# Cross attention with four key groups: products, evictions and small sums placed in other steps of the slot

## The reference, cut to what matters

```
q = heads(x @ to_q_w)
h_g = softmax(q @ heads(ctx_g @ to_k_g_w)^T / sqrt(32)) @ heads(ctx_g @ to_v_g_w)   for g in txt, obj, oth, ip
out = merge(h_txt) + merge(h_obj) + merge(h_oth) + merge(h_ip)
out = out @ to_out_w + to_out_b + x
```

## Time and profile before

| | us |
|---|---|
| median of 3 runs (2660.23 to 2662.57) | 2661.45 |
| the profiled execution's own time | 2661.54 |
| its span, first to last instruction | 2659.5 |
| PE matmul busy / weight loads busy | 2547.6 / 1936.9 |
| ACT busy | 1726.6 |
| DVE busy | 1622.1 |
| POOL busy | 408.5 |

### The profile page before, as it was taken

One profiled execution on the slowest core, in us unless ns is written; L12 is line 12 of the kernel. 1 busy time (PEld: TensorE's weight loads), 2 busy tenths in 40 slices (PEclk: granted clock), 3 DMA queues, 4 the chain that ended last, 5 costly groups with the idle time before them and its releaser, 6 DMA issues.

```text
span 2659.5 us, 37570 instructions
## 1 busy us (share of the span) xinstructions
PE 2547.6 (96%) x13221; PEld 1936.9 (73%) x13221; DVE 1622.1 (61%) x2964; ACT 1726.6 (65%) x3832; POOL 408.5 (15%) x564
## 2 busy tenths in 40 slices
PE   7999999999999947999999999999999999999997
PEld 7999999999999934566666666666666666666664
DVE  3131111111111138888888888888888888888882
ACT  3232212212121117999999999999999999999993
POOL 0000000000000022122122122221221221221210
PEclk9999999999999978999999999999999999999999
DMA  7473333332323246566666566666666666666642
GB/s 213 131 228 130 118 114 116 108 117 106 120 103 119 79 110 134 106 134 139 126 139 142 117 146 138 118 145 140 121 139 140 126 134 134 135 138 127 137 99 65
DMA packets 256918, 341.14 MB, mean 128 GB/s; under 512 B 48466, under 2 KB 150994, under 8 KB 256730
## 3 DMA queue, kind: packets, MB, share of 16 engines
q1 hardware_dynamic: 203312, 275.82, 45.4%
q10 hardware_dynamic: 53418, 62.93, 6.7%
HBM read 186.60 MB, written 83.89 MB: 102 GB/s over the span
## 4 chain that ended last, share of the span: by engine, by line
PE 41%; DVE 14%; issue 5%; ACT 4%; DMA 0%; SPq 0%; DVEq 0%
PE m_ps L838 11%; PE s_ps L766 8%; PE o_ps L794 8%; PE m_ps L815 7%; PE st_ps L780 7%; DVE negmax L949 4%; DVE q_out L1000 2%; ACT probs L885 2%; DVE small L956 2%; DVE q_out L997 2%; DVE heads L1010 2%; ACT s_ps L893 2%; DVE heads L1015 1%; DVE neglse L982 1%; DVE neglse L980 0%
## 5 line engine op out<-in xcount | busy, mean ns | idle before, releaser
L893 ACT ACTIVATE s_ps<-s_ps,negmax 128x427 f32<-128x427 f32 x1280 | 761.4, 599 | 69.7 <-DVE small L956 69.5
L949 DVE TENSOR_REDUCE negmax<-s_ps 128x2 f32<-128x854 f32 x640 | 663.2, 1036 | 146.9 <-PE s_ps L766 145.5
L885 ACT ACTIVATE probs<-st_ps 128x1024 f32<-128x1024 f32 x640 | 662.1, 1035 | 87.8 <-PE st_ps L780 87.8
L766 PEld LDWEIGHTS s_ps<-kpack,qpack 96*128 96x128 f32 x1280 | 348.4, 312 | 203.9 <-issue 114.6
L766 PE MATMUL s_ps<-kpack,qpack 96*128 96x512 f32 x1280 | 450.2, 434 | 35.9 <-ACT s_ps L893 29.2
L433 PE MATMUL v_ps<-w_split,ctx_split 128*128 128x320 f32 (+2 forms) x3168 | 467.5, 309 | 0.0
L433 PEld LDWEIGHTS v_ps<-w_split,ctx_split 128*128 128x128 f32 (+2 forms) x3168 | 461.2, 183 | 4.7 <-issue 0.5
L416 PE MATMUL k_ps<-ctx_split,w_split 128*128 128x428 f32 (+1 forms) x2280 | 431.1, 350 | 8.3 <-DVE k_out L361 8.3
L416 PEld LDWEIGHTS k_ps<-ctx_split,w_split 128*128 128x128 f32 x2280 | 413.0, 189 | 23.8 <-issue 9.3
L780 PE MATMUL st_ps<-qpack,kpack 104*128 104x512 f32 x1280 | 410.2, 402 | 9.1 <-ACT probs L885 6.1
L361 DVE TENSOR_TENSOR k_out<-k_ps,k_out 128x427 fp32r<-128x427 f32 (+1 forms) x97 | 56.3, 581 | 540.0 <-ACT k_out L257 540.0
(11 more groups left out here) (54 smaller groups left out, 1458.5 us busy)
## 6 DMA issues: line engine op xcount, KB each, us to landing
kpack<-kT SPq DMA_DIRECT2D x240, 256.0 KB, 5.4
qpack<-q_out SPq DMA_DIRECT2D x240, 256.0 KB, 5.6
kT<-k_out ACTq DMA_DIRECT2D x160, 217.5 KB, 2.2
ctx_split_raw<-in_ctxT SPq DMA_DIRECT2D x128, 214.0 KB, 4.6
xs_raw<-in_xT SPq DMA_DIRECT2D x80, 256.0 KB, 5.7
out<-in_xT SPq DMA_DIRECT2D x80, 256.0 KB, 6.0
out_yT<-out SPq DMA_DIRECT2D x80, 256.0 KB, 3.3
v_ip_rows<-v_out ACTq DMA_DIRECT2D x48, 320.0 KB
```

Source lines behind the costliest of these rows:

```text
L766: last = nc.tensor.matmul(s_ps[:, n % 2, z, :], queries_of(r, j, t), kpack[0:ROWS_S, r, j, :], start=True, stop=True)
L885: nc.scalar.activation(probs[:, at:at + 2, :], st_ps[:, :, :], ACT.Exp).then_inc(p_done, 1)
L893: last = nc.scalar.activation(s_ps[:, n % 2, z, SMALL:TOK], s_ps[:, n % 2, z, SMALL:TOK], ACT.Exp, bias=negmax[:, r, IP, j, t:t + 1], accu ...
L949: nc.vector.tensor_reduce(negmax[:, r, IP, j, t0:t0 + 2], s_ps[:, n % 2, :, SMALL:TOK], AX_X, ALU.max, negate=True).then_inc(s_max, 1)
```

## The change

Nothing that is computed changes. The steps of PE's `queries` move from 5, 6, 7 to 6, 7 and step 0 of the next slot; those of `output` from 1, 2, 3 to 2, 3, 4. `values` moves from steps 0, 2, 4, 6 to steps 1, 3, 5, 7: in 3 and 7 it stays between the transposed scores and the other products, in 1 and 5 it comes last, behind the plain scores. On DVE `keep_queries` moves from step 0 to 1, `small_sums` of the second half from 1 to 0, `add_output` from 4 to 5. POOL's splits of x take one step later names. The ring of probabilities grows from six to eight slices, and `out` shrinks from two buffers to one.

```diff
-OR = 2
+OR = 1
 HR = 9
-PR = 6
+PR = 8
@@
-Q_STEPS = {5: (0, 7), 6: (7, 9), 7: (9, 15)}
-X_STEPS = {0: (0,), 1: (1,), 2: (2,), 3: (3,), 5: (4,)}
+Q_STEPS = {6: (0, 6), 7: (6, 9), 0: (9, 15)}
+X_STEPS = {1: (0,), 2: (1,), 3: (2,), 5: (3,), 6: (4,)}
@@
-Y_STEPS = {1: (0, 6), 2: (6, 8), 3: (8, 15)}
+Y_STEPS = {2: (0, 6), 3: (6, 9), 4: (9, 15)}
@@ PE
             def products_at(m, k):
 
-                if k in Q_STEPS and unit(m):
-                    queries(m, range(*Q_STEPS[k]))
+                u = m if k > 0 else m - 1
+                if k in Q_STEPS and unit(u):
+                    queries(u, range(*Q_STEPS[k]))
@@ PE, slot
                         scores_t(u, duo)
-                    if k % 2 == 0 and unit(m - 4):
+                    if k in (3, 7) and unit(m - 4):
                         values(m - 4, k // 2)
                     products_at(m, k)
                     u, p = pair_at(m, k + 1) if k + 1 < STEPS else pair_at(m + 1, 0)
                     if unit(u):
                         scores(u, p)
+                    if k in (1, 5) and unit(m - 4):
+                        values(m - 4, k // 2)
@@ DVE, slot
-                    if k == 0 and unit(m - 1):
+                    if k == 0 and unit(m - 3):
+                        small_sums(m - 3, 1)
+                    if k == 1 and unit(m - 1):
                         keep_queries(m - 1)
-                    if k == 1 and unit(m - 3):
-                        small_sums(m - 3, 1)
@@ DVE, slot
-                    if k == 4 and unit(m - Y_LAG):
+                    if k == 5 and unit(m - Y_LAG):
                         add_output(m - Y_LAG)
```

## The result

The kernel after takes 2750.9 us (median of 4 runs, 2747.5 to 2753.3) against 2661.7 for the kernel before (4 runs, 2660.2 to 2662.6). The ratio is 1.0331, with an interval of 1.0319 to 1.0344. The forecast said slower, by 33 us; it is slower by 89, and 2750.9 lies outside the range of 2664 to 2714. The profiled execution has a span of 2745.6 us, 86.1 more than before's 2659.5.

What follows compares the result with a forecast made beforehand. PE, ACT and DVE nearly level at 19.96 us a slot; after, a 20.44 us loop through the query packing. Steady slots 20.8 more, start 8, tail 4.3: 33 us on 2661.54, so 2694 us, range 2664 to 2714.

Steps and rivals of the forecast that it cites:

- the loop: One slot long: packing waits for eviction, eviction for products, products for pair 0, pair 0 for packing; 20.44 us against 19.96.
- the packing of 8.2 us: From SP's first packing issue to pair 0 of the unit: 8.2 us, bounds 8.0 and 8.5, against PE's 7.57 of work.
- the price of a wait: PE's wait for the packed queries, counted as its own length only; no clock loss was forecast.
- the start: The nine intervals before 1153.46, 177.6 us before: 8 us more, three of the 19.11 kind losing 1.3 each.
- The rival of other traffic or the logsumexp rows: Residual, x chunks or logsumexp rows make the packing 0.6 us longer: 47 us more, 2740 us; chance 0.08.
- slots with a new x: The 14 steady slots in which POOL splits a new x: 20.64 us each, 0.43 less than 21.07.
- the 19.11 kind: Early slots in which no output is made yet, 19.11 us before; three of them were to lose 1.3 us each.
- the sign I named, nearly the same period with and without outputs: Period between issues of L652 is 20.3 to 20.6, nearly the same with and without outputs, if the forecast is right.
- The tail, "4.3 more": Last outputs with one `out` buffer: 5.7 us apart instead of 4.62, four times, 4.3 us more.
- The rival in which the collision only moves to another chunk: POOL's split of the third chunk meets DVE's logarithms fully, by the lock: 8 us more, 2702 us; chance 0.10.
- Were this all, a slot would last some 19.7 us: The steady slot from the changes to PE's list and the eviction stall alone, without the packing loop: some 19.7 us.
- 0.24 us less for each slot: On PE, two pairs of scores behind a `values` become transposed pairs, 0.10 to 0.11 against 0.23 each: 0.24 us less.

Runs made afterwards that it cites:

- the shorter third transfer: The kernel after with the last of the three packing transfers cut to 128 of 512 tokens from unit 4 on: 2678.6 us, ratio 1.0064 against the kernel before.

## Why the prediction was wrong in size, step by step

The way and the loop were right. The time failed on three terms: the packing of 8.2 us, which took 8.43 and in 20 of 70 slots 9.0 to 9.2; the price of a wait beyond its own length, put at nothing; and the start, 8 us for 23.6.

- **The loop, right.** Four of its five terms came out within 0.02 us, L766 waits for the packing once in every steady slot, and taking the loop away by the third transfer brings the period to 20.10.
- **The term "first issue of the packing to pair 0: 8.2", mis-sized.** It measured 8.43 in an ordinary slot, so the typical period is 20.69 instead of 20.44. In 14 of the 70 slots it is 9.03, and in six more 9.23. No step of the forecast asked what else uses the DMA engines. The earlier trace rows had the sign of it: the packing at 1800.23 with its landing of 7.2 has a `q8` instruction transfer beside it, the one at 1840 with 6.8 has none. The other 0.3 us of each packing go with the logsumexp rows, whose transfers SP now issues 2.8 us behind the first packing issue instead of 5.1. Over the twelve kernels with three whole transfers the first two land alike (4.2 and 6.3 after the first issue, medians of the units without a `q8` transfer). The third lands after 8.0 to 8.1 in the seven kernels that issue the rows 5.1 us or more behind, after 8.24 where it is 4.8, and after 8.4 to 8.5 in the four where it is 2.4 to 2.8. No run moved these rows alone, so this is a strong hint and not a proof. The rival of other traffic or the logsumexp rows (0.6 longer in every slot, 2740, chance 0.08) came nearest to the time: half its size for the rows, and a traffic it did not name on top.
- **The price of a wait, left out.** The forecast counted a wait as its own length. In six steady slots the wait (1.3 to 1.6 us) was followed by a fall of the granted clock, and the slot took 23.05. The 70 intervals add up: 20.8 forecast; 50 at 20.69 instead of 20.44 add 12.2; 14 at 21.28 add 11.8; 6 at 23.05 add 15.6; and 2.8 go off, since slots with a new x are no longer than the others. That is 57.6.
- **The start, "8 more", three times too small.** 23.6 us. In the four intervals of units 4 to 7 PE waits 1.5 to 1.6 us for the packing, has a clock of 0.85 to 0.92, and they last 22.2 to 23.6 us instead of the 20.4 that I gave those of the 19.11 kind. Filled with useless products they come to 20.5 to 20.7. So the sign I named, nearly the same period with and without outputs, was missed: those without are the slower ones, by the clock.
- **The tail, "4.3 more", right by mechanism.** The buffer alone costs 3.5 us between the medians. The kernel after lost 8.0 behind its last packing; one of its store intervals is 6.20 (2725.71 to 2731.91), and there PE's products took 5.27 us instead of 3.68.
- **Slots with a new x, right and better.** The 1.40 us are gone and the 14 penalties of 1.1 with them. The Trainium skill ("SBUF — State Buffer", Who interferes with whom) holds DVE and GpSimd to an exclusive lock on a port pair; moving one split of GpSimd by two steps took the longest logarithm step from 1399 to 285 ns and 14 us from the whole, which agrees. The rival in which the collision only moves to another chunk did not come.
- **"Were this all, a slot would last some 19.7 us", wrong.** With the loop open it is 20.1 to 20.2. The failed step is "0.24 us less for each slot": it saw that two pairs of scores no longer stand behind a `values`, and not that they now stand directly behind a transposed pair. From the pair at the end of step 0 to the output's first product PE needs 3.44 us (1842.04 to 1845.48) where I had 3.07; the same groups without that first pair take 3.03 in step 5 with the shorter third transfer (1818.34 to 1821.37) where my terms give 2.60. With 19.55 for the list before, my estimate from these rows is 19.55 - 0.24 + 0.37 + 0.43 = 20.11, and 20.10 was measured. The forecast's time did not suffer, because the loop was longer than either number: that was luck. It also explains the stall of the output's products, which shrank from 21.7 to 7.2 us over the run (the idle time of L838): PE now gets there later.
- **Step by step pricing, a gap.** I priced the moves of values and of the products one by one at about nothing. Alone they cost 178 and 199 us. That most of it cancels when both are made was nothing that my working showed.

Left open: why six waits of 1.3 to 1.6 us were followed by a lower clock and others of the same length were not (1.51 at 1854.69 was not); what places the instruction transfers and how they hold up a packing; whether the logsumexp rows are what makes the third landing 0.3 us later. No run removed the instruction transfers; they only moved, and the late landings with them.

## What to carry to other kernels

Before moving work along a software pipeline, draw the loop that each hand-over closes and give a transfer that nobody hides its longest landing, not its middle one. Price each group by the neighbours that it will have, not only by those that it leaves. Count a wait of PE at more than its length where its slots are nearly full: it can cost the clock as well. Pieces that together even out the steps of an engine with a one-deep buffer behind it are one edit, and their best part (here the later split) may well be had without the rest.

## What was unexpected of the hardware

- A PE that is otherwise over 90% busy showed a granted clock of 0.69 over the 5.2 us after a single wait of 1.41 us (2271.31 to 2276.51), which costs 1.5 us more of busy time. The same wait at 1434.84 cost nothing.
- Adding 75 products to the kernel made it 22 us faster.
- A single instruction transfer of 16 KB goes with a packing that is complete about 0.6 us later: 20 of 20 late packings in the steady part have one (8.71 to 9.33 us against 8.29 to 8.49), and in the run with filled early slots both moved to other units together.
- A pair of plain scores directly behind a transposed pair took 0.79 us from start to start, against 0.47 where products stand between them (1843.13 to 1843.92 and 1826.22 to 1826.69 in the kernel after).
